# Self-attention of a decoder layer on one core: where a projection's four chunks stand around the head turn

## What is computed

```python
def _L0_attn_ref(x, W_qkv, W_out, b_out):
    qkv = jnp.einsum('ble,ef->blf', x, W_qkv)
    qkv = qkv.reshape(b, l, NUM_HEADS, HEAD_DIM, 3)
    q, k, v = (qkv[0], qkv[1], qkv[2])          # after moveaxis
    q = q * cos + _rotate_half(q) * sin
    k = k * cos + _rotate_half(k) * sin
    mask = (j <= i) & (j >= i - WINDOW)         # WINDOW = 128
    scores = jnp.einsum('bhid,bhjd->bhij', q, k) * scale
    attn = jax.nn.softmax(jnp.where(mask, scores, jnp.finfo(scores.dtype).min), axis=-1)
    out = jnp.einsum('bhij,bhjd->bhid', attn, v)
    return jnp.einsum('ble,ef->blf', out, W_out) + b_out
...
x = x + _L0_attn_ref(_layernorm(x, axis=-1), L0_attn_W_qkv, L0_attn_W_out, L0_attn_b_out)
x = x + _L0_xattn_ref(_layernorm(x, axis=-1), ctx_2048, L0_xattn_Wq, L0_xattn_Wk, L0_xattn_Wv)
x = x + _L0_ffn_ref(_layernorm(x, axis=-1), L0_ffn_router_weight, ...)
```

## Time and profile before

| what | value |
|---|---|
| median of 3 runs | 1760.61 us (1759.91 to 1761.31) |
| the profiled execution | 1763.67 us, its span 1761.87 us |
| TensorE busy over the span | 1443.3 us (82%) |
| VectorE, ScalarE, GpSimd busy | 1052.7, 980.6, 771.0 us |
| first scores of self-attention, end of the stage | 43.40 us, about 515 us |
| mean granted clock of TensorE, 1 being 2.4 GHz | 0.914 |

### The profile page before, as it was taken

The page is one execution under the profiler, slowest core; times in us unless marked ns, Lnnn a source line. Parts: engine busy times, 40 slices in busy tenths (PEclk is TensorE's granted clock), DMA queues, the critical chain, the costliest instruction groups (busy, mean ns, idle before and its releaser), DMA issues. The chain is left out here.

```text
span 1761.9 us, 28899 instructions
## 1 busy us (share of the span) xinstructions
PE 1443.3 (82%) x9667; PEld 1066.1 (61%) x9667; DVE 1052.7 (60%) x2102; ACT 980.6 (56%) x1982; POOL 771.0 (44%) x494
## 2 busy tenths in 40 slices
PE   3988898989966578988988856672999999999990
PEld 2777776777744444444444323242899999999880
DVE  4667576666636524344444453445888888888880
ACT  3555454545532246755755733431777787777770
POOL 2444343443432024434434400001577777777762
PEclk9999899989987989999999976775999999999995
DMA  8000000000012581691681670033799999999986
GB/s 308 1 25 13 13 25 25 13 13 25 7 36 72 116 147 56 116 188 37 111 180 35 110 123 1 4 128 120 212 300 291 301 301 296 296 299 288 294 169 120
DMA packets 133108, 229.82 MB, mean 130 GB/s; under 512 B 17865, under 2 KB 51145, under 8 KB 132496
## 3 DMA queue, kind: packets, MB, share of 16 engines
q1 hardware_dynamic: 103184, 154.98, 32.3%
q0 software_dynamic: 29248, 72.53, 18.6%
q10 hardware_dynamic: 576, 0.98, 0.2%
HBM read 163.78 MB, written 71.83 MB: 134 GB/s over the span
## 5 line engine op out<-in xcount | busy, mean ns | idle before, releaser
L1038 ACT ACTIVATE shared<-xa_ring 128x1024 f32<-128x1024 f32 x256 | 247.2, 1029 | 142.9 <-PE xa_ring L1420 142.6
L1000 POOL TENSOR_TENSOR shared<-shared,xa_half 128x32 f32<-128x32 f32 x24 | 130.3, 5429 | 244.7 <-DVE shared L1159 244.7
L282 POOL TENSOR_TENSOR sa_prob<-sa_prob,sa_rinv 128x1024 f32<-128x1024 f32 x64 | 121.3, 1896 | 247.5 <-DVE sa_rinv L445 247.5
L1587 POOL DMA_INDIRECT ex_xg<-xn,token x128 | 169.3, 1322 | 86.5 <-issue 56.8
L340 ACT ACTIVATE sa_prob<-sa_sc_ps,sa_nmax 128x256 f32<-128x256 f32 x256 | 118.0, 473 | 113.4 <-DVE sa_nmax L432 113.4
L75 PE MATMUL ex_ba<-ex_xh,ex_wh 128*128 128x256 f32 x512 | 150.8, 295 | 5.8 <-DVE ex_xl L1701 3.7
L1432 PE MATMUL xa_out<-shared 128*17 128x512 f32 x1024 | 148.4, 654 | 0.6 <-ACT shared L1038 0.4
L76 PE MATMUL ex_ba<-ex_xl,ex_wh 128*128 128x256 f32 x512 | 146.1, 285 | 0.0
L77 PE MATMUL ex_ba<-ex_xh,ex_wl 128*128 128x256 f32 x512 | 146.0, 285 | 0.0
L1688 DVE TENSOR_TENSOR ex_wl<-shared,ex_wh 128x1024 fp32r<-128x1024 f32 (+1 forms) x128 | 116.9, 955 | 41.0 <-ACT ex_wh L1631 40.9
L432 DVE TENSOR_REDUCE sa_nmax<-sa_sc_ps 128x2 f32<-128x512 f32 x128 | 83.1, 687 | 67.6 <-PE sa_sc_ps L577 67.6
(11 more groups left out here) (235 smaller groups left out, 4024.4 us busy)
## 6 DMA issues: line engine op xcount, KB each, us to landing
shared<-in_L_ffn_gate_proj_dram SPq DMA_DIRECT2D x64, 384.0 KB
shared<-in_L_ffn_up_proj_dram SPq DMA_DIRECT2D x64, 384.0 KB
turned<-stage SPq DMA_DIRECT2D x64, 256.0 KB, 2.8
shared<-in_L_ffn_down_proj_dram SPq DMA_DIRECT2D x64, 256.0 KB
xa_kT<-turned SPq DMA_DIRECT2D x96, 128.0 KB, 7.3
xa_qT<-turned SPq DMA_DIRECT2D x96, 128.0 KB, 9.0
shared<-in_L_ffn_down_proj_dram SPq DMA_DIRECT2D x64, 128.0 KB
sa_x<-in_x_dram SPq DMA_DIRECT2D x16, 256.0 KB, 2.8
```

Source lines behind the costliest of these rows:

```text
L282: pool.tensor_tensor(prob[:, 4 * g:4 * g + 4, :], prob[:, 4 * g:4 * g + 4, :], rinv[:, 4 * g:4 * g + 4].unsqueeze(2).to_broadcast([P, 4, 2 ...
L1000: pool.tensor_tensor(power[:, i], ms[:, i], half[:], ALU.pow).then_inc(s_pw, 1)
L1038: act.activation(prob[:, w % 2, 2 * i:2 * i + 2, :], ring[i][:], ACT.Exp, scale=D2 ** -0.5).then_inc(s_ex[i], 1)
L1587: pool.indirect_dma_start(out=xg[:, e % RING, j, :], out_offset=None, in_=xn3, in_offset=bass.IndirectOffsetOnAxis(token[:, at:at + 1], 0))\
```

## The change

One line of TensorE's `tile` is different. Of the four chunks of a projection two now stand ahead of `turn_heads` and two behind it, where it was three and one. This holds for all four steps, in all tiles.

```diff
-                    for part in (range(C - 1), range(C - 1, C)):
+                    for part in (range(C // 2), range(C // 2, C)):
```

## The result

The changed kernel takes 1781.97 us (median of four, 1778.57 to 1782.89) against 1760.26 for the kernel before (median of four, 1757.4 to 1761.31): a ratio of 1.0122, 95% interval 1.0104 to 1.0141. It is slower by 21.7 us where 6.8 were forecast. The time lies within the stated range, but the size was missed threefold.

What follows compares the result with a forecast made beforehand. Self-attention was taken as bounded by TensorE, busy 89%, save where it waits. 18.9 + 0 + 4.6 - 16.7 = +6.8 us took the profiled 1763.67 to 1770.5, carried over to 1767.4 us; range 1764 to 1784 us.

Steps and rivals of the forecast that it cites:

- The turn is bound by the copy: In self-attention, the head turn waits for ACT's copy to pT out of its PSUM bank, starting 0.14 us after it ends.
- Steps 0 and 1: TensorE waits at the head turn, so these steps grow from 6.21 to 6.91 us: 27 by 0.70, +18.9 us.
- Step 2: The same 0.70 us wait is paid out of the 2.46 us idle for kT, which becomes 1.76: 0.
- Step 3: TensorE waits 0.30 us at the head turn in tiles 1 to 13, 0.70 in tile 14: +4.6 us.
- The clock: Step 3 of eight tiles: clock falls after step 2's idle time all go as the longest gap shrinks to 1.76 us, -16.7 us.
- rival 1: The clock falls in step 3 stay: +21.1 us, 1781.7 us, or +27.6, 1788 us, if five other tiles fall too; chance 0.17.
- The carry-over from the profiled execution: Whole kernel: the plain runs' median lies 3.1 us under the profiled execution, carried over from 1770.5 to 1767.4 us.

Runs made afterwards that it cites:

- the other bank: Changed kernel with the q heads of steps 0 to 2 turned into another PSUM bank, xT_ps: 1753.15 us, ratio 0.9939 to before.
- The kernel with steps 0 and 1: Kernel before with two chunks and two in steps 0 and 1 only, three and one kept in steps 2 and 3: 1786.9 us, ratio 1.0156.
- the longer one: Changed kernel with six more matmuls, result unused, at the end of step 1 of tiles 0 to 13: 1792.66 us, ratio 1.0163 to before.
- the filled kernel: Changed kernel with eight more matmuls, result unused, at the end of step 2 of tiles 0 to 13: 1766.81 us, ratio 1.0051 to before.
- the kernel with the early copy and the other bank: Kernel before with DVE's kT copy ahead of the normalisation and q heads of steps 0 to 2 turned into xT_ps: 1714.49 us, ratio 0.9744.
- both copies early: Kernel before with DVE's copy to kT ahead of both low_qk and the normalisation in step 2: 1713.6 us, ratio 0.973.
- step 3 alone: Kernel before with two chunks and two in step 3 only: 1757.79 us, ratio 1.0013.
- the early copy alone: Kernel before with DVE's copy to kT ahead of the normalisation in step 2: 1731.26 us, ratio 0.9814.

## Why the prediction was wrong, point by point

- **The turn is bound by the copy, 3.95 us into the step.** Right, to 0.01 us; shown by the other bank. The idle time ahead of it is 0.57 us where about 0.66 was named, in 47 places where some 40 were.
- **Steps 0 and 1, +18.9 us (27 by 0.70).** Right: +18.1 in the profile, with 0.7 more hidden by a fall that tile 15 no longer had. Tiles 5 and 9 paid next to nothing (7.58 and 7.75 us before, 7.75 and 7.68 now).
- **Step 2, 0.** Right; the wait for kT went from 2.46 to 1.78 us.
- **Step 3, +4.6 us at full clock.** Nearly: 0.25 us a tile instead of 0.30, since the turn follows the copy at 3.87 us here; tile 14 paid 0.70.
- **The clock, -16.7 us.** This is the step that failed. Nine falls of 1.36 us over 6.85, 12.2 us, stand in the place of the 16.7 of before, so the term was -4.5, and that only because none of the nine is as long as the three steps of 9.5 us of before. With it the sum is 23.5 - 4.5 = +19.0 against 17.5 of the spans. The mistake was to take the longest gap for what decides. Its own rows spoke against that: tiles 1, 2, 3, 6 and 7 had the same idle 2.46 us and no fall. The kernel with steps 0 and 1 has the old gap and 12 falls instead of 8, the longer one has the new gap and one fall, and in the changed kernel itself one and the same gap is followed by either. What decides it stays open. The prediction's rival 1 (the falls stay, +21.1) is what happened, but that its time, 1781.7 us, is so near the measured 1781.97 is luck: the spans differ by 17.5 us only, and the other 4 us are which executions were profiled. For it the prediction cited the Trainium skill ("TensorE: Matmul & The Clock Gate", "A second HAM failure mode: psum-queue depth-cycling"), by which frequent short gaps make the clock swing. The outcome agrees but not that reason: the filled kernel keeps all gaps of 0.57 us and has no falls.
- **The carry-over from the profiled execution.** The profiled execution was 3.1 us over the median, and its eight falls were taken as what every execution has. 25 runs of before on one chip went from 1748.7 us (mean granted clock 0.920) to 1766.7 (0.911), so the slower ones spent more time at 1.2 GHz; in which stage is not known. Where the falls of before were taken away by filling the idle time, 15.0 us were won at the median, so 16.7 was about the size.
- **The range.** It held, thanks to rival 1, but its likely value did not deserve 0.58.

## What to carry to other kernels

Before moving work away from ahead of a wait, measure how much of the wait it covers: the instruction that would wait may show no idle time at all, and a place where the same wait is bare (here the last tile, without projections) gives its length. When the clock of TensorE falls in some repetitions of a loop and not in others, do not book its return as a gain; here the same idle time was followed by a fall in some tiles and not in others, and a kernel in which the idle time is filled or gone gives the price of the change without it. The idle time that the change could only shorten, the wait for kT, was worth more than any order of the chunks: DVE's copy moved forward by one and by two operations took 30 and 49 us off, part of the latter through the jumps.

## What was not expected of the hardware

The idle time of 3.2 to 3.8 us at the loop's two jumps, for which the profile names no releaser, is not fixed. Around it the DMA queue of instructions loads. Between 165 and 380 us the kernel before shows

```profile
q8 instruction: 17, 0.28, 0.6%
```

(packets, MB, share), and in the kernel with the early copy and the other bank that queue has no row in the same stretch. With both copies early it has none either, with the other bank alone it is 1 packet, and with step 3 alone, where one of the two idle times is gone, 8. Step 3 of tile 8 ends with the jump; first the kernel with the early copy alone, then the one with the early copy and the other bank:

```profile
278.70:288.90 10.20, 6.66 (x54) 5.41 (x55) 5.40 (x9) 5.05 (x13) 3.44 (x3) 0.97 0.08 29
...
273.18:279.93 6.75, 6.67 (x55) 5.43 (x56) 5.32 (x9) 5.05 (x13) 2.18 (x2) 1.00 0.00 0
```

TensorE is busy 6.66 and 6.67 us in both; the difference of 3.45 us is the idle time, and in most cases a slow step of up to 9 us (6.2 at full clock) follows it. Both jumps together cost 8.3 us in the profile of the changed kernel, 9.6 in that of before and 11.6 in that of the early copy alone. The idle time was gone in three kernels (the other bank alone, both copies early, early copy and other bank), and in the one with step 3 alone it was gone at the first jump and there at the second. So it looks as if the loop's code is sometimes loaded again at a jump and sometimes not; that TensorE's idle time is the wait for this load is argued from the packets and not shown. What decides it is open: the kernel with both copies early has the same TensorE program as the kernel before. No experiment was made on it. It can be one reason for the spread of the executions, but their profiles are not there to show it.
